# Local attention scores and key projection each in one piece, and the lower query weights moved from GpSimd to VectorE

## What is computed

```python
def attn_layer(x, Wqkv, qs, ksc, Wo):
    q, k, v = split(x @ Wqkv)                 # 16 heads of 64
    q, k = l2norm(q) * qs, l2norm(k) * ksc
    q = q * cos * scale + rotate_half(q) * sin * scale
    k = k * cos * inv + rotate_half(k) * sin * inv
    return local_attention(q, k, v) @ Wo      # windows of 32, one looked back

def ffn_layer(x, g, bln, W1, b1, W2, b2):
    a, gate = split(layernorm(x, g, bln) @ W1 + b1)
    return a * gelu(gate) @ W2 + b2

for i in range(6):
    x = attn_layer(shift_tokens(x), ...) + x
    x = ffn_layer(shift_tokens(x), ...) + x
return x_in + attention(xn) + x
```

## Time and profile before

| what | value |
|---|---|
| median of 3 runs | 1665.17 us (1661.12 to 1668.48) |
| the profiled execution's own time | 1664.71 us |
| its span | 1662.6 us |
| granted TensorE clock | 0.999 of full |
| PE busy | 1603.9 us, 96% |
| DVE busy | 1352.6 us, 81% |
| POOL busy | 1305.1 us, 78% |
| ACT busy | 1178.3 us, 71% |

### The profile page before, as it was taken

One profiled execution on the slowest core, in us unless ns is written; L12 is line 12 of the kernel. 1 busy time (PEld: TensorE's weight loads), 2 busy tenths in 40 slices (PEclk: granted clock), 3 DMA queues, 4 the chain that ended last, 5 costly groups with the idle time before them and its releaser, 6 DMA issues.

```text
span 1662.6 us, 70904 instructions
## 1 busy us (share of the span) xinstructions
PE 1603.9 (96%) x29520; PEld 1226.0 (74%) x29520; DVE 1352.6 (81%) x1879; ACT 1178.3 (71%) x1784; POOL 1305.1 (78%) x1257
## 2 busy tenths in 40 slices
PE   8999989999999999999999999999999999999998
PEld 5777866667677777777777777776777777777777
DVE  6677867888788888788888788888788888888886
ACT  5788846677677677677677767767777776776774
POOL 6423158888888898888899888889888998888884
PEclk9999999999999999999999999999999999999999
DMA  6211113433333443334343334343334433333333
GB/s 173 59 43 41 51 27 92 113 84 98 96 76 92 106 101 92 92 90 107 84 99 89 88 93 110 86 104 85 87 93 112 97 95 90 83 75 82 80 83 75
DMA packets 128205, 146.42 MB, mean 88 GB/s; under 512 B 58256, under 2 KB 71312, under 8 KB 127120
## 3 DMA queue, kind: packets, MB, share of 16 engines
q1 hardware_dynamic: 127296, 141.43, 34.7%
q10 hardware_dynamic: 592, 0.46, 0.1%
HBM read 25.43 MB, written 1.05 MB: 16 GB/s over the span
## 4 chain that ended last, share of the span: by engine, by line
PE 60%; SPq 16%; DVE 11%; POOL 6%; issue 5%; ACT 2%; DMA 0%; POOLq 0%; DVEq 0%; ACTq 0%
PE banks L1474 37%; SPq L454 12%; PE banks L1734 6%; PE banks L1781 6%; PE banks L1851 5%; PE banks L1624 4%; DVE small L1296 1%; POOL arena L675 1%; DVE arena L1249 1%; DVE small L1278 1%; DVE arena L1244 1%; DVE small L1272 1%; POOL arena L726 1%; POOL arena L720 1%; DVE small L1284 1%
## 5 line engine op out<-in xcount | busy, mean ns | idle before, releaser
L670 POOL TENSOR_TENSOR arena<-arena 128x1024 f32<-128x1024 f32 x96 | 230.3, 2399 | 49.6 <-DVE arena L1249 44.5
L1296 DVE TENSOR_REDUCE small<-banks 128x16 f32<-128x1024 f32 x96 | 117.5, 1224 | 181.5 <-PE banks L1781 180.1
L954 ACT ACTIVATE vst<-banks 128x1024 f32<-128x1024 f32 x192 | 196.5, 1023 | 87.9 <-PE banks L1474 58.0
L1244 DVE TENSOR_TENSOR arena<-banks,tabs 128x1024 f32<-128x1024 f32 x192 | 233.4, 1215 | 3.5 <-ACT arena L910 3.5
L1249 DVE TENSOR_TENSOR arena<-banks,tabs 128x1024 f32<-128x1024 f32 x192 | 233.3, 1215 | 0.0
L675 POOL TENSOR_TENSOR arena<-arena 128x1024 f32<-128x1024 f32 x96 | 229.0, 2386 | 0.0
L665 POOL TENSOR_TENSOR prob<-prob,small 128x1024 f32<-128x1024 f32 x95 | 182.4, 1920 | 19.1 <-DVE small L1286 18.5
L720 POOL TENSOR_TENSOR arena<-arena,small 128x1024 f32<-128x1024 f32 x96 | 186.2, 1940 | 7.5
L726 POOL TENSOR_TENSOR arena<-arena,small 128x1024 f32<-128x1024 f32 x96 | 183.0, 1906 | 9.2
L1851 PE MATMUL banks<-arena 128*32 128x128 f32 x6144 | 188.5, 274 | 1.5 <-issue 1.0
L1474 PE MATMUL banks<-qkH,xsH 128*128 128x512 f32 x384 | 175.2, 456 | 9.8 <-DVE arena L1249 4.4
(11 more groups left out here) (197 smaller groups left out, 3717.2 us busy)
## 6 DMA issues: line engine op xcount, KB each, us to landing
arena<-vst SPq DMA_DIRECT2D x1536, 64.0 KB, 2.0
qkraw<-in_wqk_dram SPq DMA_DIRECT2D x11, 512.0 KB
arena<-in_wvo_dram SPq DMA_DIRECT2D x5, 1024.0 KB
tabs<-in_tab_dram SPq DMA_DIRECT2D x40, 128.0 KB, 2.6
gq<-w1w SPq DMA_DIRECT2D x58, 64.0 KB, 2.0
MH<-w1w SPq DMA_DIRECT2D x56, 64.0 KB, 2.0
lns<-Xt SPq DMA_DIRECT2D x94, 32.0 KB
lns<-Xt SPq DMA_DIRECT2D x94, 31.8 KB
```

Of the source, the lines that this page charges most:

```text
L670: pool.tensor_tensor(kc, kc, ks, ALU.add).then_inc(s["k_add"], 1)
L954: act.activation(vst[:, g, :], two(V_BANK), ACT.Copy).then_inc(s[f"v_cp{g}"], 1)
L1244: dve.tensor_tensor(heads(c), heads(two(0)), table(k % NT, kind), ALU.mult).then_inc(s[done], 1)
```

## The change

The order of calls on PE is changed: up_gate(chunk_at(G, 10), 0) and next_shifts now stand ahead of transpose_probs, the four parts of the scores follow each other (with the once-a-layer products of next_products_upper still between the second and the third), and both halves of the keys stand together behind layer_columns. The lower query weights of layers 1 to 5 are computed by DVE ahead of its maxima, and no longer by POOL; those of layer 0 stay on POOL.

```diff
-            def lower_query_weights(l):
-                pool.wait_ge(s["wq_H"], l + 1)
-                pool.tensor_tensor(query_L, qkraw[:, :] if l else query_raw0, query_H, ALU.subtract).then_inc(s["wq_L"], 1)
+            def first_query_weights():
+                pool.wait_ge(s["wq_H"], 1)
+                pool.tensor_tensor(query_L, query_raw0, query_H, ALU.subtract).then_inc(s["wq_L"], 1)
...
-            def next_query_weights(k):
-                if is_tile(k) and k % TILES == TILES - 1 and k < LAST_TILE:
-                    lower_query_weights(k // TILES + 1)
-
...
                 row_shifts(G - 5)
-                next_query_weights(G - 1)
                 next_table(G - 2)
...
+            def next_query_lower(k):
+                if is_tile(k) and k % TILES == TILES - 1 and k < LAST_TILE:
+                    dve.wait_ge(s["wq_H"], k // TILES + 2)
+                    dve.tensor_tensor(query_L, qkraw[:, :], query_H, ALU.subtract).then_inc(s["wq_L"], 1)
+
...
                 next_folded_upper(G - 2)
+                next_query_lower(G - 1)
                 maxima(G - 2)
...
                 up_value(chunk_at(G, 11), 0)
+                up_gate(chunk_at(G, 10), 0)
+                next_shifts(chunk_at(G, 12))
                 transpose_probs(G - 3)
-                up_gate(chunk_at(G, 10), 0)
                 scores_a(G - 2)
                 scores_b(G - 2)
                 next_products_upper(G - 2)
                 scores_c(G - 2)
-                if G:
-                    project_keys_first(G)
-                next_shifts(chunk_at(G, 12))
                 scores_d(G - 2)
                 layer_columns(chunk_at(G, 13))
                 if G:
+                    project_keys_first(G)
                     project_keys_last(G)
```

More of the change, by code:

```diff
@@ L586, in _ @@
             rounded(query_raw0, query_H, "wq_H")
-            lower_query_weights(0)
+            first_query_weights()
             pool.wait_ge(s["wq_L"], 1)
```

## The result

The changed kernel is slower. Its median is 1677.92 us over 14 runs (1670.26 to 1692.04), that of the kernel before 1667.95 us over 14 runs on the same chip; the ratio of the two is 1.0070, with a 95% interval of 1.0046 to 1.0094. By the ratio that is 11.7 us more (the two medians alone lie 10.0 us apart), where 14 us less were forecast. The time lies outside the range of 1636 to 1665 us.

What follows compares the result with a forecast made beforehand. PE was taken as the bound, with SyncE's DMA queue a stream of nearly equal length. 23.5 + 3 + 7.5 + 3 - 13 - 10 = 14 us off the profiled 1664.71 gave 1651 us, range 1636 to 1665.

Steps and rivals of the forecast that it cites:

- scores and keys in one piece, and the earlier maxima: PE, 94 steps: one island of key products saves 0.25 us each, 23.5 us; less waiting for scaled probabilities, 3 us.
- gate products ahead of the transposes: PE, 22 chunks: three gate products follow at pace, 0.34 us saved each, 7.5 us faster (4 to 8).
- lower query weights on DVE: Five layer starts: 1.5 us wait for POOL goes, keys scaled later; net 3 us gained (-5 to +7.5).
- bias products moved up: PE, five layers: next_shifts behind the value products waits 2.6 us for DVE's gated product; 13 us lost (10 to 14).
- DMA queue's share of the gains: SyncE's DMA issues, nearly as long a stream as PE's, take 10 us of PE's savings (bounds 0 and 31).
- well below 41: Sign of being right: SPq's waits fall well below 41 us and its chain share rises above 16%.
- rival (c): Bias-product stall decides, island savings under about 10 us: 5 + 1 - 13 - 5 = -12, 1677 us; chance 0.08.
- (a): The DMA queue doesn't bind, buffers take up its lag, PE's savings count in full: 27 us, 1638 us; chance 0.24.
- (b): The DMA queue takes nearly all of PE's savings, little left but the stall: 1 us gained, 1664 us; chance 0.20.
- 0.07 for slower: Chance given to a measurably slower kernel, against 0.70 for faster (under 1656.8 us) and 0.23 for the same.

Runs made afterwards that it cites:

- queue light: Kernels with one of the four transfers of each value block left out from the fourth tile on, so attention output is not the reference's; kernel before so: 1657.90 us.
- light kernel before: The kernel before with one of the four transfers of each value block left out from the fourth tile on: 1657.90 us, ratio 0.9962.
- light pair: For one piece: light kernel before, 1657.90 us, and the same with scores and keys in one piece alone, 1646.31 us, ratio 0.9886.
- the pairs: Kernel before against changed kernel with bias products behind the scores: 11.3 us apart in full form, 17.3 with the queue light (1657.90 and 1640.61 us).
- light changed kernel: The changed kernel with one of the four transfers of each value block left out from the fourth tile on: 1662.30 us, ratio 0.9980.

## Why the prediction was wrong, point by point

What each term measured, in us (plus is a gain; each measured value is good to 3 to 6 us):

| term | prediction | alone, full queue | queue light |
| --- | --- | --- | --- |
| scores and keys in one piece, and the earlier maxima | 23.5 + 3 | 6.0 | 12.6 |
| gate products ahead of the transposes | 7.5 | 6.5 | 6.3 |
| lower query weights on DVE | 3 | 0.7 | not tried |
| bias products moved up | -13 | -22.3 | -20.6 |
| DMA queue's share of the gains | -10 | in the column | about -6 in the full kernel |
| sum | 14 | -9.1 (whole change: -11.7) | -1.7 (whole change: -3.0) |

**The step that turned the sign: "Cost: 5 x 2.65 = 13 us".** The place, the count, the releaser and the length of the waits were right (13.9 us in five waits of 2.69 to 3.11, released by DVE L1349). What failed is that the wait was taken for its whole price. PE was priced at its full clock behind an idle time for which the earlier trace rows show no equal within a busy stretch: the longest wait of PE in them is 1.47 us, and the kernel before ran at 0.999. The trace did hold a warning, the 1.73 us wait at 425.81 with 3.2 us at the lower clock behind it. Behind the 2.7 us the granted clock was at its lower level for 3.4 or 6.8 us. What the five steps lost beyond the waits is 20.7 - 13.9 = 6.8 us in the changed kernel, 7 us in its light form (22.1 - 14.9, against the light kernel before), and 11 us in the kernel before with this one move (25.5 - 14.1). Filling the wait gave 13.3 us for the same steps at full clock, so this part is shown, not argued. The move alone costs 22.3 us where 13 were taken, and with 13 the whole change would have been near 0, not slower: this term turned the sign, the next one took the gain. The bound "10 to 14" had no upper end for what a wait of a length unseen in the trace may set off.

**The largest term: "I take 0.25 a step", 23.5 us, and 3 us for the maxima.** The islands of the keys got cheaper as forecast; three other things did not hold.

- The scores were sized by a fast instance. The 96 scores of the earlier trace rows took 1.10 us to the next product; over the loop of the kernel before they take 1.22 in the median and 1.23 in the mean, the 32 behind them 0.43 in the mean, 1.66 together. In one run of 128 they take 1.73 in the mean in the kernel with one piece alone, 1.6 in the median, and 2.1 or more in one step of ten. So the scores did not get up to 0.08 us cheaper but 0.07 dearer.
- The keys were nearly right in the usual step: six products in 1.61 us in the median (1.58 in the rows below) against medians of 0.89 + 0.90 before, 0.18 to 0.20 saved. But in some steps they stretch, at the lower clock or in a wait, and in the mean of the 43 plainest steps only 0.08 us is left. Taken together, from the first score to the turned keys, the mean over 80 steps fell by 0.06 us, where 0.25 was taken: 94 x 0.06 is 6 us, what the full kernel with one piece alone measured. In the light pair it fell by 0.136, or 13 us, again as measured.
- The scores' extra time is, where the trace can name it, "issue": PE waits for nothing that the profile shows. That happens in 14 places for 11.9 us with one piece alone, against 7 for 5.1 before. It is tied to the place in the program: in the kernel with the bias products behind the scores such waits of over 1 us end at 339.5, 398.1, 635.1 and 1439.8 us, in its light form at 340.2, 399.3, 633.5 and 1431.4. That instructions come too late there is a guess.
- The earlier maxima brought little: PE's wait for the probabilities went from 10.6 to 9.8 us (7.8 with one piece alone).

The timeline of PE in an undisturbed step of the changed kernel, against the earlier trace rows:

```profile
1084.91 1.78 PE L1782 MATMUL banks<-arena 64*32 64x64 f32 x128
1086.62 0.49 PE L1475 MATMUL banks<-qkH,xsH 128*128 128x512 f32 x1
...
1087.87 0.40 PE L1475 MATMUL banks<-qkH,xsL 128*128 128x512 f32 x1
1088.20 0.71 PE L1735 MATMUL banks<-cst,arena 64*128 64x64 f32 x16
```

**The DMA queue, 10 us: right in kind, near in size.** It takes about 6 us (17.3 against 11.3 between the pairs, and hardly clear of noise). Its chain share rose as forecast, from 16 to 25%; its waits did not fall "well below 41": in the row 40.0 us in the changed kernel, with 9.9 us of a new wait for PE beside it, and 34.2 with the bias products behind the scores. The sign that moved was ScalarE's wait for landings, from 21.4 to 43.7 us (39.9 with the bias products behind the scores), which the prediction had not read. With 6 in place of 10 the sum would have been 18, further from the result.

**Gate products: right**, 6.5 and 6.3 us against 7.5 (the rows of the prediction give 1.89 - 1.53 = 0.36 a chunk, where 0.34 was taken).

**Lower query weights: mechanism right, size within its uncertainty.** The port was the thing to fear, and it shows in the fourth layer's start, on DVE and POOL, then PE (against the earlier trace rows):

```profile
920.70 3.30 POOL L720 TENSOR_TENSOR arena<-arena,small 128x1024 f32<-128x1024 f32 x1
921.03 1.21 DVE L1324 TENSOR_TENSOR qkL<-qkraw,qkH 128x1024 fp32r<-128x1024 f32 x1
```

```profile
924.06 0.71 PE L1735 MATMUL banks<-cst,arena 64*128 64x64 f32 x16 [1.34 <-POOL arena L720]
```

The scaling of the keys took 3.30 us instead of 1.90, longer by more than the 1.21 us of DVE's whole operation and not by a part of it, and PE waited 1.34 us for it where 0.95 had been taken (the prediction's own 919.85 - 918.98 is 0.87). This was one of five layer starts, where 2.5 to 3 us had been forecast for each. At two others it was DVE's turn: its 1.2 us operation took 2.0, beside a POOL operation of 1.90 that had begun first. At the remaining two a small POOL operation ahead of the scaling took 0.9 us instead of 0.25. The Trainium skill, "SBUF — State Buffer", says in its part on the engines' port that such a pair excludes each other for the whole instruction; the 3.30 us row agrees better with that than with the partial overlap the sum was made with. The Trainium skill says in the same place that the one which starts first gets the port; by the records POOL began first here (920.70 against 921.03) and was still the longer one.

**The rivals.** The time came out where rival (c) had it, 1677 us, and half by its mechanism: the savings of the islands did stay under 10 us. The other half was missing, since it priced the stall at 13 and needed the gate products at 1 and the weights at -5 to come there. That it met the time is chance. Rivals (a) and (b) differed in the queue alone, which turned out to be neither the whole story nor nothing.

**The chance.** The stall had been found by following each moved instruction to what it waits for, and it was the one loss in a list of gains. Three of the gains rested on one row each while the loss had a bound of 14 us; 0.07 for slower was too little for that.

What stays open: why PE stands still in the runs of scores with no wait that the profile names, and more often with sixty products added elsewhere; how much of the missing one-piece gain is the queue's and how much the clock's; and whether the weights on DVE are worth 3 us once PE is shorter.

The version that beats both kernels is the changed one with the bias products behind the scores: 1653.01 us, 0.9932 of the kernel before.

## What to carry to other kernels

A new wait of some us on the matmul engine costs more than its length when the engine's clock falls behind it (here 0.6 to 2.7 us more on 2.7 to 3.1), so an instruction whose input isn't ready should stand behind everything that is; check each moved instruction for that before adding up gains. Size a saving that is repeated 94 times by the median and the mean over all its instances, not by one row, and where two streams are nearly equal in length look at who waits for the second one's results. And idle time ahead of an operation says nothing on what its being late would cost.

## What the runs showed of the hardware

- Behind 2.7 to 3.1 us in which PE did nothing, the granted clock stood at 1.2 GHz for 3.4 or 6.8 us, five times of five in the changed kernel and in the kernel before with that one move (up to 10 us in the light changed kernel); twelve products without a use in the idle time kept it at 2.4 GHz in the same places. On top of each wait that cost 0.6 to 2.7 us in the step. The Trainium skill, "TensorE: Matmul & The Clock Gate", Part 1, says that TensorE's clock is halved when the engine has been idle and given back when it has been busy; the trace agrees.
- Shorter waits of PE did the same, but seldom. Counted over the loops of all sixteen kernels here, the lower clock followed within 4 us behind 17 of 17 waits of 2.66 us and more, 12 of 21 between 1.75 and 2.5, 7 of 41 between 1.5 and 1.75, and 5 of 158 between 0.8 and 1.5.
- In a run of 128 small products (weights loaded for each) PE stands still now and then for up to 2.9 us with no semaphore behind it, 9 to 20 times in the kernels with one run of 128, against 4 to 7 times in those with runs of 96 and 32 (7 in the kernel before), and once in the one with two runs of 64.
- A GpSimd operation and a DVE operation with both inputs in SBUF took 3.30 us and 2.0 us instead of 1.90 and 1.2 when one began within the other.
